# Layer 2 of a four-layer network: turning and weighing move ahead of the projections

## The chip, the cores and the metric

One core of a Trainium2 chip runs the whole program. The metric is device time in microseconds (us) for one execution. A core has five engines that each work through their own instructions in program order and meet only at semaphores: TensorE (PE, matmuls into PSUM), VectorE (DVE), ScalarE (ACT), GpSimd (POOL) and SyncE (SP, which issues transfers).

## The reference

Four layers follow one another, each `x = x + layer(groupnorm(x))`, on 8 images of 32 x 32 tokens with 256 channels. The change is in layer 2, neighbourhood attention with 8 heads of 32 channels and a 7 x 7 window:

```
q, kk, v = split(x @ qkv_w.T + qkv_b)
k_nb, v_nb = the 7 x 7 neighbours of each token (window shifted inside the image)
attn = softmax(einsum('bnijd,bniajcd->bnijac', q * scale, k_nb) + bias)
out = einsum('bnijac,bniajcd->bnijd', attn, v_nb)
out = out @ proj_w.T + proj_b
```

## The kernel before

A tile is 4 x 4 tokens with all 8 heads (128 rows of queries) against the 10 x 10 = 100 keys around it. A step handles 4 tiles, so an image has 16 steps and the layer 128 steps, numbered N over the layer and n within image b. `Tiles` holds the attention pipeline of a step:

- `scores(N)`, TensorE, line 1735: queries against the window of keys, 8 matmuls of 100 columns.
- `add_and_low(N)`, VectorE, line 1773: adds the bias, takes the row extreme; then `exps(N)`, ScalarE, line 1793.
- `invert(N)`, VectorE, line 1779, one step later; then `scale(N)`, GpSimd, line 1800.
- `turn(N)`, TensorE, line 1746, two steps later: transposes the weights into PSUM; `copy_turned(N)`, VectorE, line 1785, copies them to SBUF (PT).
- `weigh(N)`, TensorE, line 1761, three steps later: 32 small matmuls of 16 columns, weights times values, into two PSUM banks that hold half an image.

After 8 weighings ScalarE's `copy_out` (line 2070) moves these banks to `OT`, at n == 10 for the first half and at n == 2 of the next image for the second. The semaphore `o_copied` counts these copies. `weigh` waits for it before the first step of each half (it would overwrite the banks), and `project_out` waits for it before it reads `OT`:

```
if N % (STEPS // 2) == 0 and N > 0:
    pe.wait_ge(self.o_copied, HALVES * (N // (STEPS // 2)))
```

Between the attention work, TensorE does the projections of the next image and the output projection of this one, through a ring of two PSUM banks (`Ring`), one item a step: queries at n = 0, 1 (second half of this image) and 8, 9 (first half of the next), line 1944; the output projection at 3, 4 and 14, 15; values at 4 to 7; keys at 10 to 13 (the last three through helper lines 299 and 307). ScalarE takes the queries out of the ring (`to_blocks`, line 2052, four instructions each) and the values (line 2061), directly behind the exponentials of the same step; VectorE takes the keys (line 2005) and adds the output projection to the residual (line 2012). At n = 0 VectorE measures the next image's group statistics (`moments`, line 384). At the end of step n = 10 and n = 2 ScalarE's order is exponentials, then `copy_out`.

The order of the work on each engine is the order in which these loops are written. Layer 3 uses the same `Tiles`, with its own loop, in which TensorE turns and weighs directly behind the scores and VectorE copies the turned weights before its other work.

Of the kernel before, what the change touches and what calls it, by code (L numbers as in the profile page):

```python
# [11 lines left out]
B, SIDE, C = 8, 32, 256  # L12
# [282 lines left out]
def project(nc, out, w, act, m, n0, n1):  # L295

    tiles = w.shape[1]
    for k in range(tiles):
        i = nc.tensor.matmul(out, w[:, k, m * P:(m + 1) * P], act[:, k, n0:n1], start=(k == 0), stop=(k == tiles - 1))  # L299
    return i  # L300


def project_tokens(nc, out, act, w, t):

    tiles = w.shape[1]
    for k in range(tiles):
        i = nc.tensor.matmul(out, act[:, k, t * P:(t + 1) * P], w[:, k, :], start=(k == 0), stop=(k == tiles - 1))  # L307
    return i
# [122 lines left out]
STEPS = T // TILE ** 2 // STEP  # L431
# [1382 lines left out]
def edge(t):  # L1814
    return 0 if t == 0 else 2 if t == BANDS - 1 else 1
# [26 lines left out]
def layer2(nc, A, x, y, vimg):  # L1842
    with ExitStack() as ctx:
# [16 lines left out]
        w = Tiles(L, keys, SIDE, vimg, 8)  # L1860
# [11 lines left out]
        with nc.Block() as block:  # L1872
            @block.vector
            def _(dve):
                nc.vector.tensor_tensor(bias[:, :, :], bias[:, :, :], window[:, :, :], ALU.add)
                vstep(dve, nc.vector.tensor_scalar(qkv_b[:, 0:HALVES], qkv_b[:, 0:HALVES], HD ** -0.5, None, ALU.mult))
# [8 lines left out]
        with nc.Block() as block:  # L1885
# [41 lines left out]
            @block.tensor  # L1927
            def _(pe):
                def values(b, j):
                    name = ("v", b, j)  # L1930
                    pe.wait_ge(xn_ready, 4 * b + 2 * (j // 2) + 2)
                    ring.may_fill(pe, name)
                    for t in range(2):
                        i = project_tokens(nc, ring.region(name)[:, t * C:(t + 1) * C], xn, wqkv[:, :, 2 * C:3 * C], 2 * j + t)
                    i.then_inc(ring.filled(name), 1)

                def queries(b, half, g):
                    name = ("q", b, half, g)
                    pe.wait_ge(xn_ready, 4 * b + 2 * half + 2)
                    ring.may_fill(pe, name)  # L1940
                    for q in range(4):
                        for k in range(HALVES):
                            band = xn[:, k, (4 * half + q) * P:(4 * half + q + 1) * P]
                            i = nc.tensor.matmul(ring.region(name)[:, q * P:(q + 1) * P], wqkv[:, k, g * P:(g + 1) * P],
                                                 band.rearrange("p (r t c) -> p t r c", r=TILE, c=TILE), start=(k == 0),
                                                 stop=(k == HALVES - 1))
                    i.then_inc(ring.filled(name), 1)

                def unit(name, m, half):
                    pe.wait_ge(xn_ready, 4 * name[1] + 2 * half + 2)  # L1950
                    ring.may_fill(pe, name)
                    project(nc, ring.region(name), wqkv, xn, m, half * BANK, (half + 1) * BANK).then_inc(ring.filled(name), 1)

                def project_out(b, half, m):
                    name = ("out", b, half, m)
                    pe.wait_ge(w.o_copied, 4 * b + 2 * half + 2)
                    ring.may_fill(pe, name)
                    project(nc, ring.region(name), wo, OT, m, half * BANK, (half + 1) * BANK).then_inc(ring.filled(name), 1)

                norm.average(nc, pe, ring, 0)  # L1960
                for j in range(4):
                    values(0, j)
                for g in range(HALVES):
                    queries(0, 0, g)
                for u in range(4):
                    unit(("k", 0, u), HALVES + u % 2, u // 2)
                for N in range(B * STEPS + 3):
                    b, n = N // STEPS, N % STEPS
                    if b < B:
                        if n % 8 == 0:  # L1970
                            for g in range(HALVES):
                                ring.is_taken(pe, ("q", b, n // 8, g))
                        if n == 0:
                            for u in range(4):
                                ring.is_taken(pe, ("k", b, u))
                        w.scores(nc, pe, N)
                        if n < 2:
                            queries(b, 1, n)
                        if n == 1 and b + 1 < B:
                            norm.average(nc, pe, ring, b + 1)  # L1980
                    if n in (3, 4) and 0 < b < B:
                        project_out(b - 1, 1, n - 3)
                    if b + 1 < B:
                        if 4 <= n < 8:
                            values(b + 1, n - 4)
                        if n in (8, 9):
                            queries(b + 1, 0, n - 8)
                        if 10 <= n < 14:
                            unit(("k", b + 1, n - 10), HALVES + (n - 10) % 2, (n - 10) // 2)
                    if n >= 14 and b < B:  # L1990
                        project_out(b, 0, n - 14)
                    if 2 <= N < B * STEPS + 2:
                        w.turn(nc, pe, N - 2)
                    if N >= 3:
                        w.weigh(nc, pe, N - 3)
                for m in range(HALVES):
                    project_out(B - 1, 1, m)

            @block.vector
            def _(dve):  # L2000
                def to_image(b, u):
                    name = ("k", b, u)
                    ring.is_full(dve, name)
                    g, half = u % 2, u // 2
                    nc.vector.tensor_scalar(keys[b % 2][:, g, half * BANK:(half + 1) * BANK], ring.region(name),
                                            qkv_b[:, HALVES + g:HALVES + g + 1], None, ALU.add).then_inc(ring.took(name), 1)

                def residual(b, half, m):
                    name = ("out", b, half, m)
                    ring.is_full(dve, name)  # L2010
                    s = slice(half * BANK, (half + 1) * BANK)
                    nc.vector.scalar_tensor_tensor(norm.x(b)[:, m, s], ring.region(name), proj_b[:, m:m + 1],
                                                   norm.x(b)[:, m, s], ALU.add, ALU.add).then_inc(ring.took(name), 1)

                def table(N, i):
                    _, tr, tc = w.tile(N, i)
                    return bias[:, 3 * edge(tr) + edge(tc), :]

                norm.moments(nc, dve, vstep, 0)
                norm.collect(nc, dve, ring, 0)  # L2020
                for u in range(4):
                    to_image(0, u)
                for N in range(B * STEPS + 2):
                    b, n = N // STEPS, N % STEPS
                    if b < B:
                        w.add_and_low(nc, dve, N, table, 1.0)
                    if 1 <= N < B * STEPS + 1:
                        w.invert(nc, dve, N - 1)
                    if n == 0 and b + 1 < B:
                        norm.moments(nc, dve, vstep, b + 1)  # L2030
                    if n == 1 and b + 1 < B:
                        norm.collect(nc, dve, ring, b + 1)
                    if n in (3, 4) and 0 < b < B:
                        residual(b - 1, 1, n - 3)
                    if 10 <= n < 14 and b + 1 < B:
                        to_image(b + 1, n - 10)
                    if n >= 14 and b < B:
                        residual(b, 0, n - 14)
                    if N >= 2:
                        w.copy_turned(nc, dve, N - 2)  # L2040
                for m in range(HALVES):
                    residual(B - 1, 1, m)

# [785 lines left out]
```

## Time and profile before

| | |
|---|---|
| median of 3 runs | 3466.73 us (3464.69 to 3476.52) |
| profiled execution, its own time | 3469.34 us |
| its span | 3467.5 us |
| mean granted TensorE clock | 0.953 of full speed |
| TensorE matmul busy | 3105.6 us, 90% |
| VectorE busy | 2211.7 us, 64% |
| ScalarE busy | 2058.1 us, 59% |
| GpSimd busy | 1155.1 us, 33% |

The shares are means over four layers with different limits. Layer 2 lies between about 2112 and 2643 us of the span; image 3 in it, for instance, takes the 66 us from 2305 to 2371, with TensorE busy 63.7, ScalarE 40.9, VectorE 33.2 and GpSimd 17.3 us. In rows of time, a row is a start, a length, the engine and line, what is written from what, shapes and a count; what stands in brackets is how long the engine was idle before it and what ended that. A 4-pass matmul of 32-bit numbers counts as two in the trace, so a count there is twice that in the program, but for the transposes. The printed length of a group of matmuls runs a little into the next one; from one start to the next is the safer measure.

### The profile page before, as it was taken

The numbers are of one execution on the slowest core, as the hardware profiler recorded it, in microseconds if no ns is written. First come the engines' busy times: TensorE is split into PE (matmuls) and PEld (weight loads), VectorE is DVE, ScalarE is ACT, GpSimd is POOL, SyncE is SP. The second block draws the span as 40 slices with busy tenths as digits, with TensorE's granted clock in tenths as the row PEclk, the third lists the DMA queues.
The fourth block names the chain that finished last, engine by engine and source line by source line (L and its number), as shares of the span: only waits on it lengthen the run. The fifth ranks groups of instructions, "written<-read, shape, count | busy, mean of one in ns | idle before, by whom it ended". The sixth has DMA issues, their size and how long they took to land. (4 is left out here: it accounts for less than half of the span.)

```text
span 3467.5 us, 94027 instructions
## 1 busy us (share of the span) xinstructions
PE 3105.6 (90%) x38656; PEld 1750.2 (50%) x38656; DVE 2211.7 (64%) x5202; ACT 2058.1 (59%) x4412; POOL 1155.1 (33%) x1446
## 2 busy tenths in 40 slices
PE   6999999999955999999999858999994899999996
PEld 2333333333312556566656526777772566666664
DVE  5878878887733667676777533545543566666765
ACT  2667676767633555545555515656562677777774
POOL 3433434343301222222222202222222455555554
PEclk9999999999976999999999979999997999999998
DMA  6777787777852333323323214445443233333332
GB/s 201 155 173 164 157 184 173 152 174 160 170 130 68 66 86 84 83 72 86 84 71 72 74 57 139 145 143 159 145 133 128 67 93 107 107 113 113 110 95 83
DMA packets 286233, 413.94 MB, mean 119 GB/s; under 512 B 25952, under 2 KB 242800, under 8 KB 264816
## 3 DMA queue, kind: packets, MB, share of 16 engines
q1 hardware_dynamic: 263248, 270.32, 26.0%
q0 software_dynamic: 18432, 134.23, 19.4%
q8 instruction: 308, 5.05, 0.6%
q10 hardware_dynamic: 4128, 3.39, 0.3%
q14 instruction: 117, 0.96, 0.1%
HBM read 219.30 MB, written 53.81 MB: 79 GB/s over the span
## 5 line engine op out<-in xcount | busy, mean ns | idle before, releaser
L732 DVE TENSOR_TENSOR l_probs<-l_psum,l_decay 128x1024 f32<-128x1024 f32 x512 | 598.6, 1219 | 163.5 <-PE l_psum L628 152.8
L780 ACT ACTIVATE l_sizes<-l_probs 128x2048 f32<-128x2048 f32 x256 | 487.6, 1910 | 300.3 <-DVE l_probs L732 293.0
L1793 ACT ACTIVATE l_logits<-l_logits,l_low 128x100 f32<-128x100 f32 x1024 | 374.7, 369 | 238.1 <-DVE l_low L1773 237.1
L1800 POOL TENSOR_TENSOR l_logits<-l_logits,l_inv 128x400 f32<-128x400 f32 x256 | 235.0, 918 | 737.7 <-DVE l_inv L1779 736.8
L628 PE MATMUL l_psum<-l_qk 32*128 32x512 f32 x2048 | 340.6, 646 | 7.9 <-POOL l_qk L866 4.2
L881 POOL DMA_DIRECT2D l_sizes<-l_sizes x128 | 111.5, 871 | 548.1 <-ACT l_sizes L780 536.1
L1632 POOL TENSOR_TENSOR l_E<-l_E,l_causal 128x1024 f32<-128x1024 f32 x64 | 153.3, 2396 | 378.0 <-DVE l_x_act L1365 224.8
L643 PE MATMUL l_psum<-l_probs,l_V 128*32 128x512 f32 x2048 | 270.6, 600 | 1.7 <-DVE l_probs L732 1.6
L299 PE MATMUL l_psum<-l_xT,l_w_up 128*128 128x512 f32 x512 | 232.2, 607 | 12.7 <-DVE l_row_var L1423 8.6
L1735 PE MATMUL l_psum<-l_keys,l_q_blocks 128*64 128x100 f32 x4096 | 230.6, 253 | 3.7 <-issue 2.4
L2726 POOL TENSOR_SCALAR l_soft<-l_dist,l_sharp,l_border 128x100 f32<-128x100 f32 x512 | 229.0, 464 | 0.1
L628 PEld LDWEIGHTS l_psum<-l_qk 32*128 32x128 f32 x2048 | 100.9, 184 | 249.1 <-issue 190.5
L1785 DVE COPY l_PT<-l_psum 100x512 f32<-100x512 f32 x256 | 172.7, 675 | 77.9 <-PE l_psum L1746 76.4
L1761 PE MATMUL l_psum<-l_PT,l_V_windows 100*32 100x16 f32 x16384 | 196.9, 186 | 15.0 <-issue 10.8
L1735 PEld LDWEIGHTS l_psum<-l_keys,l_q_blocks 128*64 128x64 f32 x4096 | 197.5, 136 | 12.6 <-issue 4.8
L1761 PEld LDWEIGHTS l_psum<-l_PT,l_V_windows 100*32 100x32 f32 x16384 | 170.1, 111 | 64.5 <-issue 63.1
L1793 ACT ACTIVATION_READ_ACCUMULATOR l_logits<-l_logits,l_low 128x1 f32 x1024 | 194.4, 190 | 0.0
L1746 PE MATMUL l_psum<-l_ident,l_logits 128*100 128x128 f32 x1024 | 161.6, 281 | 12.0 <-POOL l_logits L1800 11.9
L1773 DVE CUSTOM_DVE_ANT_0 l_logits<-l_psum,l_bias 128x100 f32<-128x100 f32 x512 | 103.3, 258 | 99.5 <-PE l_psum L1735 99.5
L299 PEld LDWEIGHTS l_psum<-l_xT,l_w_up 128*128 128x128 f32 x512 | 97.1, 195 | 125.5 <-issue 121.2
L1500 ACT ACTIVATE l_E<-l_E,l_tok_vals 128x128 f32<-128x128 f32 x512 | 156.5, 396 | 0.9 <-POOL l_E L1632 0.9
L307 PE MATMUL l_psum<-l_w_qkv,l_xn 128*128 128x256 f32 x512 | 130.3, 404 | 18.9 <-DVE l_V L2460 12.8
(246 smaller groups left out, 6072.0 us busy)
## 6 DMA issues: line engine op xcount, KB each, us to landing
l_sizes<-l_sizes POOLq DMA_DIRECT2D x128, 1024.0 KB, 7.5
l_V_windows<-v_image SPq DMA_DIRECT2D x512, 100.0 KB
l_V_windows<-v_padded SPq DMA_DIRECT2D x512, 100.0 KB
l_E<-rows_c SPq DMA_DIRECT2D x64, 512.0 KB, 5.8
l_xT<-y SPq DMA_DIRECT2D x24, 1024.0 KB, 5.3
y<-l_res SPq DMA_DIRECT2D x32, 512.0 KB, 3.7
l_e_everywhere<-rows_e SPq DMA_DIRECT2D x112, 128.0 KB, 5.6
l_xT<-x SPq DMA_DIRECT2D x8, 1024.0 KB, 11.7
```

Of the source, the lines that this page charges most:

```text
L299: i = nc.tensor.matmul(out, w[:, k, m * P:(m + 1) * P], act[:, k, n0:n1], start=(k == 0), stop=(k == tiles - 1))
L628: i = nc.tensor.matmul(out[:, a * BANK:(a + 1) * BANK], qk[r:r + HD, g, 1, J * P:(J + 1) * P], qk[r:r + HD, g, 0, m * BANK:(m + 1) * BANK] ...
L643: i = nc.tensor.matmul(PS[a * HD:(a + 1) * HD, 6 * BANK:7 * BANK], V[:, J, h * HD:(h + 1) * HD], probs[:, N % 2, a, :], start=(J == 0), st ...
L732: nc.vector.tensor_tensor(probs[:, N % 2, 2 * p:2 * p + 2, :], ring.region(name).rearrange("p (a n) -> p a n", a=2), decay[:, h:h + 2, s0: ...
L780: nc.scalar.activation(sizes[:, slot(N), :, :], probs[:, N % 2, :, :], ACT.Abs).then_inc(sized, 1)
L1735: m = nc.tensor.matmul(self.ps[64 * g:64 * g + 64, c0 + i * NKEY:c0 + (i + 1) * NKEY], self.q[:, g, tr * BANDS + tc, :], image[:, r0:r0 + ...
L1746: m = nc.tensor.transpose(self.ps[0:NKEY, c0:c0 + P], self.logits[:, N % 4, i, :], self.ident[:, :])
L1761: m = nc.tensor.matmul(out[:, r0:r0 + TILE, tc * TILE:(tc + 1) * TILE], self.v[0:NKEY, N % self.slots, i, h * HD:(h + 1) * HD], self.pt[0: ...
L1785: nc.vector.tensor_copy(self.pt[0:NKEY, N % 2, :], self.ps[0:NKEY, (2 + N % 2) * BANK:(3 + N % 2) * BANK]).then_inc(self.pt_ready, 1)
L1793: nc.scalar.activation(e, e, ACT.Exp, scale=-1.0, bias=self.low[:, N % 4, i:i + 1], accum_out=self.total[:, N % 4, i:i + 1]).then_inc(self ...
L1800: nc.gpsimd.tensor_tensor(p, p, self.inv[:, N % 4, :].unsqueeze(2).to_broadcast([P, STEP, NKEY]), ALU.mult).then_inc(self.p_ready, 1)
L2726: m = nc.gpsimd.tensor_scalar(soft[:, M % SOFTS, i * NKEY:(i + 1) * NKEY], dist[:, :], sharp[:, b % 2, t:t + 1], border[:, b % 2, t:t + 1] ...
```

## The change

On TensorE, `turn(N - 2)` and `weigh(N - 3)` of a step now stand directly behind `scores(N)`, and the projections of the step last. On VectorE, `copy_turned(N - 2)` stands before the statistics, the keys and the residual of the step.

```diff
                         w.scores(nc, pe, N)
+                    if 2 <= N < B * STEPS + 2:
+                        w.turn(nc, pe, N - 2)
+                    if N >= 3:
+                        w.weigh(nc, pe, N - 3)
+                    if b < B:
                         if n < 2:
                             queries(b, 1, n)
...
                     if n >= 14 and b < B:
                         project_out(b, 0, n - 14)
-                    if 2 <= N < B * STEPS + 2:
-                        w.turn(nc, pe, N - 2)
-                    if N >= 3:
-                        w.weigh(nc, pe, N - 3)
...
                         w.invert(nc, dve, N - 1)
+                    if N >= 2:
+                        w.copy_turned(nc, dve, N - 2)
                     if n == 0 and b + 1 < B:
                         norm.moments(nc, dve, vstep, b + 1)
...
                         residual(b, 0, n - 14)
-                    if N >= 2:
-                        w.copy_turned(nc, dve, N - 2)
```

TensorE before, image 1, steps 8 to 11 (L1735 scores, L1944 queries, L1746 turning, L1761 weighing, L299 keys' projection):

```order
L1735 MATMUL l_psum<-l_keys,l_q_blocks 64x100 x8
L1944 MATMUL l_psum<-l_xn,l_w_qkv 128x128 x8
L1746 MATMUL l_psum<-l_ident,l_logits 100x128 x4
L1761 MATMUL l_psum<-l_PT,l_V_windows 32x4x4 x32
L1735 MATMUL l_psum<-l_keys,l_q_blocks 64x100 x8
L1944 MATMUL l_psum<-l_xn,l_w_qkv 128x128 x8
L1746 MATMUL l_psum<-l_ident,l_logits 100x128 x4
L1761 MATMUL l_psum<-l_PT,l_V_windows 32x4x4 x32
L1735 MATMUL l_psum<-l_keys,l_q_blocks 64x100 x8
L299 MATMUL l_psum<-l_xn,l_w_qkv 128x512 x2
L1746 MATMUL l_psum<-l_ident,l_logits 100x128 x4
L1761 MATMUL l_psum<-l_PT,l_V_windows 32x4x4 x32
```

And TensorE in the same place of the changed kernel:

```order
L1735 MATMUL l_psum<-l_keys,l_q_blocks 64x100 x8
L1746 MATMUL l_psum<-l_ident,l_logits 100x128 x4
L1761 MATMUL l_psum<-l_PT,l_V_windows 32x4x4 x32
L1944 MATMUL l_psum<-l_xn,l_w_qkv 128x128 x8
L1735 MATMUL l_psum<-l_keys,l_q_blocks 64x100 x8
L1746 MATMUL l_psum<-l_ident,l_logits 100x128 x4
L1761 MATMUL l_psum<-l_PT,l_V_windows 32x4x4 x32
L1944 MATMUL l_psum<-l_xn,l_w_qkv 128x128 x8
L1735 MATMUL l_psum<-l_keys,l_q_blocks 64x100 x8
L1746 MATMUL l_psum<-l_ident,l_logits 100x128 x4
L1761 MATMUL l_psum<-l_PT,l_V_windows 32x4x4 x32
L299 MATMUL l_psum<-l_xn,l_w_qkv 128x512 x2
```

In each step the projection has moved from the second place to the last, behind 4 transposes and 32 weighing matmuls.

TensorE before, image 1, from the scores of step 2 to the weighing of step 3 (there L299 is the output projection; step 2 has no projection):

```order
L1735 MATMUL l_psum<-l_keys,l_q_blocks 64x100 x8
L1746 MATMUL l_psum<-l_ident,l_logits 100x128 x4
L1761 MATMUL l_psum<-l_PT,l_V_windows 32x4x4 x32
L1735 MATMUL l_psum<-l_keys,l_q_blocks 64x100 x8
L299 MATMUL l_psum<-l_OT,l_w_proj 128x512 x2
L1746 MATMUL l_psum<-l_ident,l_logits 100x128 x4
L1761 MATMUL l_psum<-l_PT,l_V_windows 32x4x4 x32
```

And TensorE there in the changed kernel:

```order
L1735 MATMUL l_psum<-l_keys,l_q_blocks 64x100 x8
L1746 MATMUL l_psum<-l_ident,l_logits 100x128 x4
L1761 MATMUL l_psum<-l_PT,l_V_windows 32x4x4 x32
L1735 MATMUL l_psum<-l_keys,l_q_blocks 64x100 x8
L1746 MATMUL l_psum<-l_ident,l_logits 100x128 x4
L1761 MATMUL l_psum<-l_PT,l_V_windows 32x4x4 x32
L299 MATMUL l_psum<-l_OT,l_w_proj 128x512 x2
```

Step 2 keeps its order; in step 3 the first instruction that needs `OT`'s copy is now the weighing, where it was the projection.

## Rows read from the trace of the kernel before

**Rows 1.** TensorE's waits in layer 2: who waited for whom, us in total, times, longest.
```profile
PE l_psum L299 <- ACT l_OT L2070: 15.5, 8, 2.2
```

**Rows 2.** TensorE in time, image 1, steps 8 to 11: start us, length us, engine, line.
```profile
2208.41 0.91 PE L1735 MATMUL l_psum<-l_keys,l_q_blocks 128*64 128x100 f32 x16
2209.24 2.05 PE L1944 MATMUL l_psum<-l_xn,l_w_qkv 128*128 128x128 f32 x16
2211.13 0.60 PE L1746 MATMUL l_psum<-l_ident,l_logits 128*100 128x128 f32 x4
...
2212.33 0.91 PE L1735 MATMUL l_psum<-l_keys,l_q_blocks 128*64 128x100 f32 x16
...
2217.09 1.98 PE L299 MATMUL l_psum<-l_xn,l_w_qkv 128*128 128x512 f32 x4
2218.91 0.60 PE L1746 MATMUL l_psum<-l_ident,l_logits 128*100 128x128 f32 x4
2219.44 0.73 PE L1761 MATMUL l_psum<-l_PT,l_V_windows 100*32 100x16 f32 x64
2220.10 0.91 PE L1735 MATMUL l_psum<-l_keys,l_q_blocks 128*64 128x100 f32 x16
```

**Rows 3.** ScalarE in time over the same four steps.
```profile
2209.66 0.38 ACT L1793 ACTIVATE l_logits<-l_logits,l_low 128x100 f32<-128x100 f32 x1 [2.86 <-DVE l_low L1773]
...
2211.33 2.76 ACT L2052 ACTIVATE l_q_blocks<-l_psum,l_qkv_b 32x512 f32<-32x512 f32 x4
...
2215.70 2.76 ACT L2052 ACTIVATE l_q_blocks<-l_psum,l_qkv_b 32x512 f32<-32x512 f32 x4
2218.49 0.38 ACT L1793 ACTIVATE l_logits<-l_logits,l_low 128x100 f32<-128x100 f32 x1
...
2220.23 1.27 ACT L2070 ACTIVATE l_OT<-l_psum,l_qkv_b 128x512 f32<-128x512 f32 x2 [0.17 <-PE l_psum L1761]
```

**Rows 4.** TensorE, then VectorE, in time, image 7, step 15.
```profile
2625.62 0.60 PE L1746 MATMUL l_psum<-l_ident,l_logits 128*100 128x128 f32 x4
...
2625.82 0.75 DVE L2012 SCALAR_TENSOR_TENSOR l_xT<-l_psum,l_proj_b,l_xT 128x512 f32<-128x512 f32 x1 [1.00 <-PE l_psum L299]
```

**Rows 5.** TensorE in time, image 1, from step 0 to step 4.
```profile
2172.03 0.91 PE L1735 MATMUL l_psum<-l_keys,l_q_blocks 128*64 128x100 f32 x16 [0.15 <-issue]
...
2182.28 0.91 PE L1735 MATMUL l_psum<-l_keys,l_q_blocks 128*64 128x100 f32 x16
2185.38 2.98 PE L299 MATMUL l_psum<-l_OT,l_w_proj 128*128 128x512 f32 x4 [2.19 <-ACT l_OT L2070]
...
2189.99 0.91 PE L1735 MATMUL l_psum<-l_keys,l_q_blocks 128*64 128x100 f32 x16
```

**Rows 6.** ScalarE in time, image 1, steps 0 to 3.
```profile
2174.96 2.76 ACT L2052 ACTIVATE l_q_blocks<-l_psum,l_qkv_b 32x512 f32<-32x512 f32 x4
...
2184.06 1.27 ACT L2070 ACTIVATE l_OT<-l_psum,l_qkv_b 128x512 f32<-128x512 f32 x2
```

**Rows 7.** TensorE in time after the same wait in images 2 and 4.
```profile
2252.87 1.98 PE L299 MATMUL l_psum<-l_OT,l_w_proj 128*128 128x512 f32 x4 [1.94 <-ACT l_OT L2070]
...
2384.89 3.78 PE L299 MATMUL l_psum<-l_OT,l_w_proj 128*128 128x512 f32 x4 [2.17 <-ACT l_OT L2070]
```

**Rows 8.** GpSimd, then TensorE, in time, image 0, step 4.
```profile
2124.49 0.85 POOL L1800 TENSOR_TENSOR l_logits<-l_logits,l_inv 128x400 f32<-128x400 f32 x1 [0.87 <-DVE l_inv L1779]
...
2126.15 1.99 PE L307 MATMUL l_psum<-l_w_qkv,l_xn 128*128 128x256 f32 x8 [2.79 <-POOL l_xn L422]
```

**Rows 9.** TensorE in time in layer 3, one step.
```profile
2853.84 0.65 PE L1746 MATMUL l_psum<-l_ident,l_logits 128*100 128x128 f32 x4
2854.42 0.74 PE L1761 MATMUL l_psum<-l_PT,l_V_windows 100*32 100x16 f32 x64
2855.09 1.98 PE L299 MATMUL l_psum<-l_OT,l_w_out 128*128 128x512 f32 x4
2856.91 1.95 PE L2331 MATMUL l_psum<-l_xn,l_w_qkv 128*128 128x128 f32 x16
```

## The prediction

> **What bounds the kernel now.** I read the per-stage windows first, to find where the changed code runs: layer 2 takes about 531 us of the 3467.5 us span (2112 to 2643), and in seven of its eight images TensorE shows some work nearly all the time. So a change of order can win only what TensorE waits for, and can lose where it makes TensorE wait. The list of TensorE's waits over the layer has one entry that matters: the output projection (L299, reading OT) waits eight times, 15.5 us in all, for ScalarE's copy of the weighted values, line 2070 [rows 1]. The rest of the argument comes from the time view.
>
> I count time within an image from the start of the scores of step 0 or of step 8. A step with queries is 0.83 us of scores, 1.89 of queries, 0.53 of turning and 0.67 of weighing, start to start, 3.92 in all; one with a 512-column projection has 1.82 in place of 1.89 and takes 3.85 [rows 2]. TensorE goes from one to the next without a gap. ScalarE has slack in most steps (it waited 2.86 us before the exponentials of step 8), but not in steps 8 to 10 and 0 to 2: there it has two sets of queries to spread into blocks, 2.76 us each, beside its exponentials of about 1.6 us a step and the copy of 1.27 us [rows 3, 6]. Those two stretches decide the case.
>
> **Part 1: the sum of TensorE's own work.** The change adds and removes no instruction. In 110 of the 128 steps (14 in image 0, 15 in each of images 1 to 6, 6 in image 7, counted from the loop) something is projected, and there the neighbours change: before, scores, projection, turning, weighing; after, scores, turning, weighing, projection. Layer 3 already works in the new order, so its rows price it: turning behind scores 0.58, weighing 0.67, projection behind weighing 1.82 [rows 9], against 0.53, 0.66 and 1.82 now [rows 2]. Turning loses 0.05, because its first weight load no longer hides behind a long matmul. Scores now stand behind a long matmul and should win the same; layer 2 has no row for it. I take 0 for the sum. If scores win nothing, it is 110 x 0.05, about +6 us; that is the bound above. The Trainium skill, "TensorE: Matmul & The Clock Gate", section "LDWEIGHTS (loading the stationary operand)", says that a load takes its column count over 1.2 in ns, and its account of a matmul's phases that such a load hides only behind a running matmul; by that a 128-column load behind 16-column weighings costs 107 ns, an estimate of +12 us over 110 steps. Rows 9 show no such surcharge.
>
> **Part 2: steps 8 to 11, where the cost is new.** Queries are usable 0.20 us after the next instruction group starts (the same delay shows at a residual, 2625.62 to 2625.82 [rows 4]). Before, the first queries land at 0.83 + 1.89 + 0.20 = 2.92 us, exactly when ScalarE, whose exponentials began at 1.25, turns to them [rows 2, 3]. After, they land behind turning and weighing: 0.83 + 0.57 + 0.67 + 1.89 + 0.20 = 4.16. ScalarE takes its work in program order, so it idles 1.24 us with the exponentials of step 9 queued behind. Then: blocks 4.16 to 6.92; exponentials of step 9 to 8.53; blocks (the second queries land at 3.92 + 4.16 = 8.08) to 11.29; exponentials of step 10, 1.57, to 12.9; copy 1.27, to 14.17. TensorE needs that copy for the first weighing of the second half of the image, since it overwrites what the copy reads. That weighing stands in step 11, whose scores start at 11.69 [rows 2]. Before, it comes at 11.69 + 0.84 + 1.82 + 0.53 = 14.88 and the copy is over at 11.82 + 1.27 = 13.09: 1.8 us to spare, nothing waits. After, it comes at 11.69 + 0.84 + 0.57 = 13.10 and the copy is done at 14.17, seen 0.05 later: a new wait of about 1.15 us. (In the old order the copy itself waited for the last weighing of step 10 [rows 3]; that one comes earlier now, but ScalarE is not free to use it.) It happens in images 0 to 6: **+8.0 us**. ScalarE has its slack back by step 12.
>
> **Part 3: steps 0 to 3.** The same delay of 1.24 us enters at the first queries (ScalarE starts them at 2.93 now, and would at 4.16), and nothing up to the copy absorbs it: ScalarE runs without a break from there to 13.30 [rows 6]. VectorE's scores of step 1 are held by the group statistics of step 0, but those end near 5.5, before ScalarE's 6.9. Before: the copy ends at 13.30, the projection of step 3 starts at 13.35 after a wait of 2.2, and at full clock 1.82 + 0.53 + 0.67 follow, so step 4 could start at 16.37 [rows 5]. After: scores and turning of step 3 are over at 10.25 + 0.83 + 0.57 = 11.65; now the weighing waits for the copy, until 14.59, 2.9 us; 0.67 and 1.82 follow, so step 4 starts at 17.08. Turning moved ahead of the wait gives 0.53 back, the delay takes 1.24: 0.71 net, in images 1 to 7: **+5.0 us**.
>
> **Part 4: the ends.** In image 0, step 4, values wait for the normalised input until 2126.15, and turning and weighing stand behind them [rows 8]. After, turning starts when GpSimd's scaling is over (2125.34, plus 0.05), weighing ends at 2126.63, and values follow: 2126.63 against 2126.15 + 1.20, **-0.7 us**. At the layer's end the last residual, 0.75 us [rows 4], stands right before the last reciprocal, which the last turning needs: up to **+0.7 us**. VectorE's copy of the turned weights moves ahead of its projection work; TensorE waits for it nowhere now, so that gives 0. The projection work behind it reads 1.2 us later and ends at about 4.85 in its step, when the next scores are ready (4.80): covered to 0.05 us. The value stores and the window loads on SyncE are tied to values copied a step earlier and to weighings that come earlier: 0.
>
> **Part 5: the clock.** After the wait in image 1 the four projection matmuls take 2.98 us, and step 4 starts 4.61 us after them where 3.02 would do: 1.6 lost at the lower of the clock's two levels, 1.2 instead of 2.4 GHz. In image 4 they take 3.78; in image 2, after 1.94 of wait, 1.98, full clock [rows 5, 7]. By the same subtraction five of the seven images lose, 9.0 us in all by my reading of the time view. With 2.9 us of wait I expect it in nearly all seven: 7 x 1.8 = 12.6, at most +3.6, and I take **+2 us**.
>
> **Sum:** 8.0 + 5.0 - 0.7 + 0.7 + 0 + 2 = **+15 us**. The profiled execution took 3469.3 us beside a median of 3466.7; so 3484 on its scale, and 3482 as a median.
>
> **Rivals.**
> Dearer order (0.13): the clock also falls after the seven new waits of 1.15 us (7 x 1.6 = +11), or the scores win nothing and weight loads show (+6). For it: waits of about 2.2 us do it. Against: they are twice as long, and rows 9 are clean. Time 3488 to 3498.
> Clock given back (0.14): the waits move to other places, and the 9.0 us lost to the clock now are not lost again. 13 - 9 = +4: 3471, no change to be seen. For it: image 2 waited 1.94 without loss. Against: the waits get longer.
> ScalarE absorbs the delay (0.07), the one that ends faster: if the 1.24 us did not reach the copy, turning ahead of the wait gives 7 x 0.53, the wait of step 3 shrinks to 1.7 and the clock stays up (9.0), and step 11 doesn't wait: -13, so 3454. Step 3 changes sign where less than 0.53 us of delay reaches the copy. Only slack on ScalarE could do that, and in steps 0 to 2 the trace shows none.
> No effect (0.05): TensorE's total counts alone; 3467.
>
> **The numbers.** Forecast 0.61. The measurement tells a change from none at about 0.3%, 10.4 us, that is 3477. The forecast's own range is 3474 to 3488, since the sum without the clock is +13 and small terms can miss: about nine tenths of it is slower. Slower 0.61 x 0.9 + 0.13, about 0.68; same 0.06 + 0.14 + 0.05, about 0.25; faster 0.07. The range of 3464 to 3496 leaves out the faster rival and the top of the dearer one.
>
> **What would show it.** TensorE's waits: a new entry, weighing (L1761) waiting for OT's copy, fourteen times, 7 x 1.15 and 7 x 2.9, some 28 us; no projection waiting for OT except at the layer's end. ScalarE: about 1.2 us of waiting for queries (L1944) ahead of the first block copy of each pair. VectorE: reads of keys and residuals start 0.2 us after the next scores. I am wrong if the weighing of step 11 doesn't wait, if step 4 doesn't start near 17, or if a step of plain projection takes other than 3.85 us.

## The result

The changed kernel is slower: 3492.1 us as the median of 5 runs (3486.6 to 3499.7), beside 3473.3 us for the kernel before in 5 runs (3464.7 to 3476.6). The ratio is 1.0064, with a 95% interval of 1.0037 to 1.0091, so about +22 us (+13 to +32); the two medians are 18.9 us apart. That is beyond the 0.3% bound, on the side that was forecast, inside the range of 3464 to 3496, and more than the +15 of the sum: 3492.1 lies above the forecast's own 3474 to 3488 and within the 3488 to 3498 of the dearer-order rival.

The profile after, its span, TensorE's share and the row of the weighing:

```profile
span 3484.8 us, 94027 instructions
...
PE 3107.6 (89%) x38656; PEld 1737.2 (50%) x38656; DVE 2207.2 (63%) x5202; ACT 2053.2 (59%) x4412; POOL 1154.6 (33%) x1446
...
L1761 PE MATMUL l_psum<-l_PT,l_V_windows 100*32 100x16 f32 x16384 | 196.4, 186 | 38.4 <-ACT l_OT L2071 23.7
```

Over the whole program TensorE is as busy as before (3107.6 against 3105.6 us) and there are as many instructions; within layer 2 alone it is busier, 510.6 us after 497.0 (in a second pair of traces 509.5 after 494.4). New in the weighing's row is 23.7 us of idle time that ScalarE's copy to OT (now line 2071) ended.

Single runs of one kernel differ by some 0.3%, and layer 2 begins anywhere between 2098.9 and 2122.7 us in the traces below, so from here on I compare the length of layer 2 alone: from the first scores to the start of the last residual. Before it is 526.6 us (2112.23 to 2638.82), after 547.6 us (2106.10 to 2653.72): +21.0 us, and layers 0 and 1 together and layer 3 differ by 6 us the one way and 2 the other. So layer 2 alone accounts for the effect.

TensorE's waits there, as in [rows 1]:

```profile
PE l_psum L1761 <- ACT l_OT L2071: 23.7, 14, 2.8
...
PE l_psum L1746 <- POOL l_logits L1800: 3.3, 3, 2.0
PE l_psum L299 <- ACT l_OT L2071: 1.4, 1, 1.4
```

Fourteen waits of the weighing have taken the place of seven of the eight of the output projection; the eighth, at the layer's end, stays. TensorE over image 1, steps 8 to 11, then two steps further on one whole step with a keys' projection (compare [rows 2]):

```profile
2206.25 0.91 PE L1735 MATMUL l_psum<-l_keys,l_q_blocks 128*64 128x100 f32 x16
...
2210.44 0.91 PE L1735 MATMUL l_psum<-l_keys,l_q_blocks 128*64 128x100 f32 x16
...
2214.69 0.91 PE L1735 MATMUL l_psum<-l_keys,l_q_blocks 128*64 128x100 f32 x16
...
2218.68 0.91 PE L1735 MATMUL l_psum<-l_keys,l_q_blocks 128*64 128x100 f32 x16
2219.52 0.64 PE L1746 MATMUL l_psum<-l_ident,l_logits 128*100 128x128 f32 x4
2220.68 0.73 PE L1761 MATMUL l_psum<-l_PT,l_V_windows 100*32 100x16 f32 x64 [0.52 <-ACT l_OT L2071]
...
2227.40 0.91 PE L1735 MATMUL l_psum<-l_keys,l_q_blocks 128*64 128x100 f32 x16
2228.24 0.64 PE L1746 MATMUL l_psum<-l_ident,l_logits 128*100 128x128 f32 x4
2228.81 0.73 PE L1761 MATMUL l_psum<-l_PT,l_V_windows 100*32 100x16 f32 x64
2229.48 1.98 PE L299 MATMUL l_psum<-l_xn,l_w_qkv 128*128 128x512 f32 x4
2231.39 0.91 PE L1735 MATMUL l_psum<-l_keys,l_q_blocks 128*64 128x100 f32 x16
```

ScalarE over the same steps (compare [rows 3]; the bracket is the new wait for the queries):

```profile
2210.55 2.75 ACT L2053 ACTIVATE l_q_blocks<-l_psum,l_qkv_b 32x512 f32<-32x512 f32 x4 [1.48 <-PE l_psum L1944]
...
2214.91 2.76 ACT L2053 ACTIVATE l_q_blocks<-l_psum,l_qkv_b 32x512 f32<-32x512 f32 x4
...
2219.27 1.27 ACT L2071 ACTIVATE l_OT<-l_psum,l_qkv_b 128x512 f32<-128x512 f32 x2
```

The copy ends at 2219.27 + 1.27 = 2220.54, 14.29 us after the scores of step 8, where 14.17 was forecast. But the wait of step 11 is 0.52 and not 1.15 us, because TensorE is late itself: its step 11 starts 12.43 us after step 8, not 11.69. The last five rows show the cause of 0.14 us in each step (the other 0.3 us here are two longer weighings in steps 8 and 9, such as single steps of both kernels have). From scores to scores it takes 3.99 us, not 3.85: scores 0.84, turning 0.57, weighing 0.67 and the projection **1.91**, where it took 1.82.

TensorE in steps 0 to 4 of image 1 (compare [rows 5]), then ScalarE's first query copy and its copy to OT (compare [rows 6]):

```profile
2170.49 0.91 PE L1735 MATMUL l_psum<-l_keys,l_q_blocks 128*64 128x100 f32 x16
...
2180.81 0.91 PE L1735 MATMUL l_psum<-l_keys,l_q_blocks 128*64 128x100 f32 x16
...
2185.12 0.73 PE L1761 MATMUL l_psum<-l_PT,l_V_windows 100*32 100x16 f32 x64 [2.83 <-ACT l_OT L2071]
...
2187.69 0.91 PE L1735 MATMUL l_psum<-l_keys,l_q_blocks 128*64 128x100 f32 x16
```

```profile
2174.66 2.76 ACT L2053 ACTIVATE l_q_blocks<-l_psum,l_qkv_b 32x512 f32<-32x512 f32 x4 [1.35 <-PE l_psum L1944]
...
2183.71 1.27 ACT L2071 ACTIVATE l_OT<-l_psum,l_qkv_b 128x512 f32<-128x512 f32 x2
```

The weighing of step 3 waits 2.83 us (2.9 forecast) and step 4 starts 17.20 us after step 0 (17.08 forecast).

### The profile page after: what moved, and what is told of

The parts are those of the page before. It is cut to its first block and busy times, and to the rows that moved or that the text cites. A ratio compares the mean times of both kernels' runs of the same rounds, so it can differ in the third digit from the quotient of the medians.

```text
span 3484.8 us, 94027 instructions
## 1 busy us (share of the span) xinstructions
PE 3107.6 (89%) x38656; PEld 1737.2 (50%) x38656; DVE 2207.2 (63%) x5202; ACT 2053.2 (59%) x4412; POOL 1154.6 (33%) x1446
## 5 line engine op out<-in xcount | busy, mean ns | idle before, releaser
L299 PE MATMUL l_psum<-l_xT,l_w_up 128*128 128x512 f32 x512 | 231.6, 606 | 13.1 <-DVE l_row_var L1423 8.8
L1735 PE MATMUL l_psum<-l_keys,l_q_blocks 128*64 128x100 f32 x4096 | 230.9, 254 | 0.9 <-DVE l_keys L2006 0.9
L1761 PE MATMUL l_psum<-l_PT,l_V_windows 100*32 100x16 f32 x16384 | 196.4, 186 | 38.4 <-ACT l_OT L2071 23.7
L1735 PEld LDWEIGHTS l_psum<-l_keys,l_q_blocks 128*64 128x64 f32 x4096 | 198.0, 137 | 58.9 <-issue 51.7
L1761 PEld LDWEIGHTS l_psum<-l_PT,l_V_windows 100*32 100x32 f32 x16384 | 170.5, 111 | 88.0 <-issue 66.2
L1746 PE MATMUL l_psum<-l_ident,l_logits 128*100 128x128 f32 x1024 | 166.1, 285 | 14.2 <-POOL l_logits L1800 14.2
L299 PEld LDWEIGHTS l_psum<-l_xT,l_w_up 128*128 128x128 f32 x512 | 96.9, 194 | 125.9 <-issue 121.7
L652 PE MATMUL l_psum<-l_sizes,l_ones 128*32 128x512 f32 x1024 | 138.0, 611 | 9.5 <-DMA l_sizes<-l_sizes 9.5
## 6 DMA issues: line engine op xcount, KB each, us to landing
l_e_everywhere<-rows_e SPq DMA_DIRECT2D x112, 128.0 KB, 5.6
```

Of the source, the lines that this page charges most:

```text
L1735: m = nc.tensor.matmul(self.ps[64 * g:64 * g + 64, c0 + i * NKEY:c0 + (i + 1) * NKEY], self.q[:, g, tr * BANDS + tc, :], image[:, r0:r0 + ...
L1746: m = nc.tensor.transpose(self.ps[0:NKEY, c0:c0 + P], self.logits[:, N % 4, i, :], self.ident[:, :])
L1761: m = nc.tensor.matmul(out[:, r0:r0 + TILE, tc * TILE:(tc + 1) * TILE], self.v[0:NKEY, N % self.slots, i, h * HD:(h + 1) * HD], self.pt[0: ...
```

## The experiments

Layer 2 in the trace of each kernel, in the order in which they are told:

| kernel | layer 2, us | ratio to the kernel before |
|---|---|---|
| before, first and second trace | 526.6, 522.3 | |
| changed, first and second trace | 547.6, 547.4 | 1.0064 [1.0037, 1.0091] |
| e3: queries early | 550.3 | 1.0065 [1.0038, 1.0093] |
| e4: turning last | 563.9 | 1.0095 [1.0063, 1.0128] |
| e5: wide first load | 565.2 | one run, no interval |
| e1: VectorE's half alone | 540.4 | 1.0060 [1.0039, 1.0081] |
| e9: the same, not at n = 0 | 519.2 | 1.0004 [0.9982, 1.0026] |
| e2: TensorE's half alone | 554.4 | 1.0076 [1.0053, 1.0099] |
| e8: queries early, their copy late | 533.2 | 1.0040 [1.0020, 1.0060] |
| e7: changed, copy to OT first | 529.5 | 1.0035 [1.0019, 1.0050] |
| e6: before, copy to OT first | 512.4 | 0.9960 [0.9947, 0.9974] |

**The two kernels again.**

> The kernel before, once more, to see how much the length of layer 2 (from the first scores to the start of the last residual, 526.6 us in the first trace) differs from one execution to the next. Both theories expect 524 to 530: the granted clock after the seven waits for OT's copy is the only thing that should differ.

> The changed kernel once more. Layer 2 took 547.6 us in the first trace; 544 to 551 expected, again with steps of 3.99 us and with fourteen waits of the weighing for OT's copy.

Layer 2 took 522.3 and 547.4 us, so the difference is 21 to 25 us, and a single length is good to some 5 us. What differs most between the two traces of before is the granted clock behind the wait for OT's copy. In the first trace it fell to the lower of its two levels in five of the seven images (1, 3, 4, 5 and 6), in the second in one (3); image 1 did not lose there, after nearly the same wait of 2.17 us:

```profile
2183.53 1.99 PE L299 MATMUL l_psum<-l_OT,l_w_proj 128*128 128x512 f32 x4 [2.17 <-ACT l_OT L2070]
```

Compare the 2.98 us of this row's twin in [rows 5]. In the changed kernel it fell behind the wait in four of the seven images in the first trace (2, 3, 5, 6) and in five in the second (2, 3, 4, 6, 7).

**e3: only the queries early.**

```diff
                         w.scores(nc, pe, N)
+                        if n < 2:
+                            queries(b, 1, n)
+                        if n in (8, 9) and b + 1 < B:
+                            queries(b + 1, 0, n - 8)
                     if 2 <= N < B * STEPS + 2:
                         w.turn(nc, pe, N - 2)
```

The same calls are taken out behind the weighing.

> The changed kernel, with the queries alone (n = 0, 1, 8, 9) put back directly behind the scores; all other projections stay last. Theory ScalarE: the queries land at 2.9 us again, so the seven waits of step 11 go (4.4 us), and the waits of step 3 shrink from 2.8 to about 1.7 us (8 us). Theory weight load: the 30 query steps go back from 4.06 to 3.92 (4 us), the other 80 keep 3.99. With both at work layer 2 takes about 531 us; with the second alone 543; with the first alone 535.

```profile
PE l_psum L1761 <- ACT l_OT L2071: 20.2, 7, 3.4
```

The waits of step 11 are gone (7 are left of 14), and query steps are back at 3.92 us: both theories have their piece. But layer 2 is 550.3 us, not 531, and the wait of step 3 has grown to 3.4 us instead of shrinking. So something else makes step 3 late here. It took e1 to see what: VectorE's copy, moved ahead, waits for turning in step 0, and the scores of step 1 are read late.

**e4: turning last in the step.**

```diff
                         w.scores(nc, pe, N)
-                    if 2 <= N < B * STEPS + 2:
-                        w.turn(nc, pe, N - 2)
                     if N >= 3:
                         w.weigh(nc, pe, N - 3)
...
                     if n >= 14 and b < B:
                         project_out(b, 0, n - 14)
+                    if 2 <= N < B * STEPS + 2:
+                        w.turn(nc, pe, N - 2)
```

> The changed kernel, with turning put last in the step: scores, weighing, projection, turning. Theory weight load: a projection followed by scores costs 0.09 us more than one followed by turning, since the 64-column weights of the scores are not loaded behind it as the 100-column ones of turning are; so steps are 3.86 us again although the projection still stands behind the weighing, 15 us less; the waits for OT's copy stay, about 1.2 us in step 11 and 2.9 in step 3: layer 2 about 540 us. Rival, that it is the projection behind the weighing that costs (its first load has only 16-column matmuls to hide behind): steps stay at 3.99, layer 2 about 552.

One step of it on TensorE:

```profile
2214.27 0.91 PE L1735 MATMUL l_psum<-l_keys,l_q_blocks 128*64 128x100 f32 x16
2215.13 0.74 PE L1761 MATMUL l_psum<-l_PT,l_V_windows 100*32 100x16 f32 x64
2215.79 1.99 PE L307 MATMUL l_psum<-l_w_qkv,l_xn 128*128 128x256 f32 x8
2217.62 0.60 PE L1746 MATMUL l_psum<-l_ident,l_logits 128*100 128x128 f32 x4
2218.16 0.91 PE L1735 MATMUL l_psum<-l_keys,l_q_blocks 128*64 128x100 f32 x16
```

The step is 3.89 us from scores to scores (2214.27 to 2218.16), with 1.83 for the values' projection that stands behind the weighing, and 3.87 is the sum for a keys' step. So the projection's place behind the weighing costs nothing; what costs is that scores follow it. For that question the run is clean. The total of 563.9 is far over the 540 expected: the waits for OT's copy grew to 33.4 us and the granted clock fell behind the wait of step 3 in all seven images. The reason is that of e3, which e1 shows below: VectorE's copy stands first and turning now comes last in the step, so the scores of step 1 in image 1, begun at 2188.35, are read only at 2192.19. I had not put that into the expectation.

**e5: a full-width load at the head of the scores.** In each step of layer 2 the first score matmul takes 128 columns of weights, its tile's 64 and the next tile's; the next matmul overwrites the upper half of the output.

```diff
+                wide = self.side == SIDE and i == g == 0
-                m = nc.tensor.matmul(self.ps[64 * g:64 * g + 64, c0 + i * NKEY:c0 + (i + 1) * NKEY],
-                                     self.q[:, g, tr * BANDS + tc, :], image[:, r0:r0 + KEYS, k0:k0 + KEYS],
+                m = nc.tensor.matmul(self.ps[0:P, c0 + i * NKEY:c0 + (i + 1) * NKEY] if wide else
+                                     self.ps[64 * g:64 * g + 64, c0 + i * NKEY:c0 + (i + 1) * NKEY],
+                                     self.q[:, g, tr * BANDS + tc:tr * BANDS + tc + 2, :].rearrange("p t q -> p (t q)") if wide
+                                     else self.q[:, g, tr * BANDS + tc, :], image[:, r0:r0 + KEYS, k0:k0 + KEYS],
```

> The changed kernel, but in layer 2 the first score matmul of each step takes 128 columns of weights (its tile and the next) instead of 64; the second matmul overwrites the half that isn't wanted. Theory weight load, in the form that a load is only pulled ahead where it has the width of the one in use: a projection followed by scores goes from 1.91 back to about 1.82 us, the scores themselves may grow by up to 0.06: layer 2 538 to 545 us. Rival: the cost has another cause (the change of the PSUM bank or of the operand): 1.91 stays, layer 2 547 to 552.

The load of that first matmul, then TensorE from a projection to turning:

```profile
2233.40 0.19 PEld L1736 LDWEIGHTS l_psum<-l_keys,l_q_blocks 128*128 128x128 f32 x1 [0.24 <-issue]
...
2232.01 1.98 PE L299 MATMUL l_psum<-l_xn,l_w_qkv 128*128 128x512 f32 x4
2233.83 1.19 PE L1736 MATMUL l_psum<-l_keys,l_q_blocks 128*128 128x100 f32 x16
2234.95 0.64 PE L1749 MATMUL l_psum<-l_ident,l_logits 128*100 128x128 f32 x4
```

The load (2233.40) starts 0.43 us ahead of its matmul (2233.83), as the load of turning does before. The projection is back at 1.82. Without this edit, in the changed kernel:

```profile
2230.44 0.19 PEld L299 LDWEIGHTS l_psum<-l_xn,l_w_qkv 128*128 128x128 f32 x1 [0.24 <-issue]
2231.39 0.28 PEld L1735 LDWEIGHTS l_psum<-l_keys,l_q_blocks 128*64 128x64 f32 x6 [0.76 <-issue]
```

the 64-column load starts only with its matmul, 2231.39, after 0.76 us in which nothing was loaded; the median over the layer is the same, for scores behind a projection of keys or output. And in the kernel before, the load of turning behind the same projection, whose matmul starts at 2230.47:

```profile
2230.04 0.13 PEld L1746 LDWEIGHTS l_psum<-l_ident,l_logits 128*100 128x100 f32 x1 [0.24 <-issue]
```

So the difference of 0.09 us is one hidden weight load. Weights of the projection and of turning go to all 128 output partitions or to 100 of them, those of the scores to 64; a load behind a projection was pulled ahead for turning (before) and for the widened scores (e5) and not for the scores of 64. That the width decides is the plainest reading, since e5 keeps the bank and the operand and changes only how many output columns the load takes; no run varies the width further. As a repair it is worthless: the scores with the wide first matmul are 1.12 us long in place of 0.84 (2233.83 to 2234.95), 0.28 us more where I had allowed 0.06, and layer 2 takes 565.2 us in this one run.

**e1: VectorE's half alone.**

```diff
                         w.invert(nc, dve, N - 1)
+                    if N >= 2:
+                        w.copy_turned(nc, dve, N - 2)
                     if n == 0 and b + 1 < B:
                         norm.moments(nc, dve, vstep, b + 1)
```

> The kernel before, with VectorE's half of the change alone: the copy of the turned weights ahead of statistics, keys and residual. My theory: TensorE waits for that copy nowhere, so nothing changes, layer 2 524 to 530 us. Rival: the copy stands ahead of the keys and the residual, so with turning late in the step it waits for turning, and these come later; if something hangs on them, layer 2 gets longer by up to 0.1 us in each of 60 steps.

My theory was wrong: 540.4 us, and 1.0060. VectorE in step 0 of image 1 (scores at 2177.35 are those of step 1):

```profile
2176.79 0.69 DVE L1785 COPY l_PT<-l_psum 100x512 f32<-100x512 f32 x1 [1.51 <-PE l_psum L1746]
2177.40 2.46 DVE L384 BATCH_NORM_STATS2 l_gn_stats<-l_xT 128x6 f32<-128x512 f32 x4
...
2180.53 0.26 DVE L1773 CUSTOM_DVE_ANT_0 l_logits<-l_psum,l_bias 128x100 f32<-128x100 f32 x1
```

```profile
PE l_psum L299 <- ACT l_OT L2070: 19.4, 8, 3.2
```

The copy waits for turning, which in the old TensorE order stands last, and the group statistics (2.46 us) stand behind it. So the scores of step 1 are read at 2180.53, 3.18 us after they were begun. Before it was 1.53 us, and that was just when ScalarE became free [rows 6]. The output projection of step 3 then waits up to 3.2 us. The rival had the right direction but not the place.

**e9: the same, but not at n = 0** (diff against the kernel before).

```diff
                         w.invert(nc, dve, N - 1)
+                    if N >= 2 and n not in (0,):
+                        w.copy_turned(nc, dve, N - 2)
...
-                    if N >= 2:
+                    if N >= 2 and n in (0,):
                         w.copy_turned(nc, dve, N - 2)
```

> The kernel before with VectorE's half of the change in all steps but n = 0. If all the loss of VectorE's half alone (layer 2 540.4 against 526.6 and 522.3 us) comes from the statistics of step 0 that wait behind the copy, this takes 522 to 528 us. Rival, that the copy ahead of keys and residual costs something in other steps too: 530 to 540.

519.2 us and a ratio of 1.0004: the loss of e1 came from step 0. Ahead of the keys and the residual the copy costs nothing that can be seen here.

**e2: TensorE's half alone.**

> TensorE's half of the change alone; VectorE copies the turned weights last as before. VectorE reads keys and residuals about 4.2 us after the step's scores start, so its copy ends near 5.6, and the weighing of the next step stands at 5.4: my theory expects a new wait of about 0.25 us in each step with keys or output projection, 50 to 60 of them, so layer 2 about 560 us. Rival: the copy is in time anyway, and the two halves of the change are independent: 547 us as with both.

(VectorE's two moved lines are put back where they were.)

```profile
PE l_psum L1761 <- ACT l_OT L2071: 21.8, 14, 2.6
...
PE l_psum L1761 <- DVE l_PT L1785: 3.1, 7, 1.0
```

554.4 us, 7 more than with both halves. The seven waits of the second row are six of 0.3 to 0.4 us in step 1, behind the statistics of step 0, and one of 1.0 at the layer's end. The wait that I expected in the steps behind keys or a residual is there too, but it is only 0.10 us, too short for that list. Image 4, step 12, turning and weighing, then VectorE's copy between them:

```profile
2380.18 0.64 PE L1746 MATMUL l_psum<-l_ident,l_logits 128*100 128x128 f32 x4
2380.85 0.90 PE L1761 MATMUL l_psum<-l_PT,l_V_windows 100*32 100x16 f32 x64
...
2380.12 0.68 DVE L1785 COPY l_PT<-l_psum 100x512 f32<-100x512 f32 x1
```

The copy ends at 2380.80 and the weighing starts at 2380.85, 0.67 us after turning; with both halves it is 0.57. The longer distance stands in 40 steps (n = 12 to 15 and 0 nearly throughout, a few at 4), 4.0 us; with six times 0.36 and the 1.0 that is the 7 us. So the mechanism was right and its size, 0.25 us, was not; the rival, that the halves are independent, is refuted.

**e8: e3 with VectorE's old order in the query steps.** VectorE's part of the edit, against e3:

```diff
-                    if N >= 2:
+                    if N >= 2 and n not in (0, 1, 8, 9):
                         w.copy_turned(nc, dve, N - 2)
...
                     if n >= 14 and b < B:
                         residual(b, 0, n - 14)
+                    if N >= 2 and n in (0, 1, 8, 9):
+                        w.copy_turned(nc, dve, N - 2)
```

> The changed kernel, with query steps (n = 0, 1, 8, 9) wholly in the order of before, on TensorE and on VectorE: in these steps VectorE copies the turned weights last again. The earlier run with TensorE's half of this alone took 550.3 us; theory: there the copy stood ahead of the statistics of step 0 and waited for turning, so the scores of step 1 were read 1.9 us late. Then this one has no wait in step 11, a wait of at most 1.8 us in step 3, steps of 3.99 us in the 80 others (+11 us): layer 2 524 to 534 us. Rival, that queries early don't help since ScalarE isn't the cause: 545 to 551.

```profile
PE l_psum L1761 <- ACT l_OT L2073: 11.2, 7, 1.7
```

533.2 us, and no wait of step 3 above 1.7 where 1.8 was the most expected: as expected. This is the changed kernel without the delay of the queries. It is 14 us shorter than the changed one and 9 longer than the mean of before (524.4). What remains is about what the 80 steps of 3.99 us cost, 11 us.

**e7 and e6: the copy to OT ahead of the exponentials at n = 2**, in the changed kernel (e7) and in the kernel before (e6).

```diff
                     b, n = N // STEPS, N % STEPS
+                    if n == 2 and b > 0:
+                        copy_out(2 * b - 1)
                     w.exps(nc, act, N)
```

> The changed kernel with the copy to OT ahead of the exponentials at n = 2. If ScalarE's queue sets the wait of the weighing in step 3, the copy ends near 13.0 us after step 0 started and not near 14.5, so seven waits fall from 2.8 to about 1.3 us: 10 us less, and fewer drops of the clock behind them; layer 2 530 to 537 us, and the steps keep 3.99 and the waits of step 11 their 0.6 us. Against the same move in the kernel before (layer 2 512.4) it stays about 20 us longer: 15 for the steps, 4 for step 11. Rival, that the weighing waits for something else: 545 to 550.

> The kernel before, with one move on ScalarE: at n = 2 the copy to OT stands ahead of the step's exponentials. If ScalarE's queue is what the output projection of step 3 waits for, the copy starts when the last weighing is over (about 10.4 us after step 0 started) and ends near 11.7, so the wait falls from 2.2 to about 0.6 us, 7 times: -11 us, and the clock doesn't fall behind it, up to 9 more: layer 2 507 to 517 us. Rival: the exponentials of step 2 are then late and hold the turning of step 4: the wait only moves, layer 2 524 to 528.

In e7 the same fourteen waits fell from 23.7 to 12.8 us, the longest from 2.8 to 1.4:

```profile
PE l_psum L1761 <- ACT l_OT L2071: 12.8, 14, 1.4
```

and layer 2 from 547.5 to 529.5 us; the granted clock fell behind none of the seven waits of step 3, where it had fallen behind four and five. In e6 ScalarE's second query copy, its copy to OT and the projection of step 3 in image 1, and the waits of the layer:

```profile
2178.51 2.75 ACT L2052 ACTIVATE l_q_blocks<-l_psum,l_qkv_b 32x512 f32<-32x512 f32 x4
...
2181.75 1.26 ACT L2070 ACTIVATE l_OT<-l_psum,l_qkv_b 128x512 f32<-128x512 f32 x2
...
2183.07 1.98 PE L299 MATMUL l_psum<-l_OT,l_w_proj 128*128 128x512 f32 x4 [0.88 <-ACT l_OT L2070]
```

```profile
PE l_psum L299 <- ACT l_OT L2070: 6.0, 8, 1.4
```

The copy starts 0.5 us after the query copy ends. The eight waits are 6.0 us where they were 15.5, none of the seven projections of step 3 runs at the lower clock, and layer 2 takes 512.4 us. The kernel takes 3452.3 us (median of 6) beside 3467.2 (13 runs), ratio 0.9960 with an interval of 0.9947 to 0.9974. It beats both kernels. e7 against e6 leaves 17 us for what TensorE's order costs beside the wait of step 3, where 20 were expected; since in e6 the clock also fell in step 4 of image 0 (9.12 us for 6.72) and in e7 it did not, 19 to 20 us is the better figure.

## Why the prediction was right, and where it was not

**Part 1, the sum of TensorE's own work: the term that was mis-sized.** I took 0, with +6 above. It measured +0.14 us a step: turning +0.04 as read from layer 3, the projection +0.09 (1.91 for 1.82), and no gain on the scores (0.84 stays), where I had expected them to win back what turning lost. Over 110 steps that is +15 us, beyond my bound (14 us with step 15, whose weighing took 0.82 us before and 0.67 after, so that this step stayed at 4.0 in images 0 to 6; why it was longer before is not shown). A step of plain projection of 3.99 us for 3.85 is one of the three signs by which the prediction was to be called wrong; the other two, the wait of step 11 and step 4 near 17, came as forecast. The rows of e4 and e5 show why: behind a projection the load of turning is hidden and that of the scores is not, so what turning loses nobody wins. The changed order has one hidden load less in every step. My row for the projection (2855.09 to 2856.91 [rows 9]) had another full-width matmul behind it, while in the changed layer the scores stand there. I had priced a group by what stands ahead of it and had not asked what stands behind it. The rule of the Trainium skill weighed there ("TensorE: Matmul & The Clock Gate", section "LDWEIGHTS (loading the stationary operand)") was applied to the projection behind the weighing; the estimate of +12 us from it comes close to the measured 15, but from another place: e4 shows 1.82 to 1.83 in that position, no surcharge.

**Part 2, steps 8 to 11: right in mechanism, too large in size.** The wait is where it was put, the copy ends within 0.12 us of the forecast, and e3 and e8 remove it. It is 0.5 to 0.7 us, not 1.15, so 4.5 us in all for 8.0 (23.7 less seven of 2.6 to 2.8). TensorE's own longer steps, which part 1 had put at nothing, hide the rest.

**Part 3, steps 0 to 3: right.** 2.6 to 2.8 us of wait for 2.9; step 4 at 17.20 for 17.08, so 0.83 us more an image than the 16.37 of an undisturbed one before, 5.8 us for 5.0. e8 shows that the delay of the queries is its cause, and e6 and e7 that ScalarE's queue is. The statement (in part 4) that VectorE's copy, moved ahead, "gives 0" held only together with TensorE's half, where it saves 7 us (e2); by itself it costs 14 to 18 us (e1).

**Part 4, the ends: nearly.** The last output projection starts 11.98 us after the scores of step 15, before 10.47 (in the second traces 11.95 and 10.57): +1.4 to +1.5 where +0.7 was the most. The last residual follows at 17.13 and before at 15.86, but at 17.11 and 17.05 in the second pair: there the clock was low for longer in the kernel before, and from that projection to the residual it took 6.48 us, beside 5.15 to 5.39 in the other three traces. In image 0 turning does wait for GpSimd's scaling, 2.04 us, and where the clock stayed up step 4 takes 5.97 us (second trace of the changed kernel) for 6.72 (first trace of before): the -0.7 as forecast. In each of the other two traces the clock fell there, and it took 8.67 and 9.21.

**Part 5, the clock: open in size.** In the kernel before, the waits of step 3 (1.6 to 2.2 us in the first trace, 1.2 to 2.3 in the second) were followed by the lower clock in five of seven images and in one; in the changed kernel the waits of 2.6 to 2.8 us were in four and in five, not in nearly all seven as expected. Steps 0 to 3 of images 1 to 7 took 2.9 us more in the first pair of traces (125.8 for 122.9) and 12.9 more in the second (128.0 for 115.2), where 5.8 would do without the clock. So the clock was worth about -3 us in one pair and +7 in the other. Their mean is the +2 that was taken, but two pairs 10 us apart cannot confirm it.

Put together at full clock: of the 89 steps outside steps 0 to 3 of images 1 to 7 all but seven steps 15 at 0.14, 11.5 us; step 11, 4.5; steps 0 to 3, 5.8; the end, 1.4; image 0, -0.7; together some 22 us. With the clock as it fell (-3 in images 1 to 7 and +2.7 in image 0 in the first pair; +7, -2.5 and, at the layer's end, -1.3 in the second) that gives 22 and 26, against 21.0 and 25.2 in the traces. The prediction's +15 is some 7 short of this, and that it came so near is in part luck, since misses partly cancelled: TensorE's own work 11.5 too low where it shows, steps 0 to 3 and the end 1.5 too low, step 11 3.5 too high (linked to the first, since longer steps eat waits), and 2 for the clock, which this sum leaves out.

**The rivals.** "Dearer order" was true in its second half (weight loads show), not in its first (no lower clock behind the short waits). Its time, 3488 to 3498, holds the measured one. "ScalarE absorbs the delay" is refuted by the copy's end at 14.29 us for 14.17 and by e8; "clock given back" and "no effect" by the measured slowdown.

## What to carry to other kernels

When instructions change places on TensorE, price each neighbourhood anew, the pair behind as well as the pair ahead: here the same four groups in another order cost 0.14 us more a step, since one weight load lost its cover, and the steps with a projection made most of the loss. When one engine's work moves later within a step, follow it into the engine that takes it up, and look for the stretch in which that engine has no slack: 1.2 us of delay there came out whole. And before an order is rewritten, look at the releaser of the largest wait: moving that one copy ahead of four exponentials gave 0.4% where reordering TensorE lost 0.6%.

## What the runs showed of the hardware

- A weight load for 64 output columns was not started while a 128-wide projection ran (load and matmul both at 2231.39, loader idle 0.76 us); one for 128 (e5) and one for 100 (turning) was, 0.43 us ahead. One matmul with 128 columns of weights ahead of seven with 64 made the scores 0.28 us longer (e5), more than the hidden load gave back (0.09).
- The same wait of 2.17 to 2.19 us was followed by projections at the lower clock (2.98 us) in one execution and at the full clock (1.99 us) in another.
- Two halves of a change, 6 and 7.6 thousandths slower each by itself, cost 6.4 thousandths together: they are not additive. With VectorE's half alone its copy waits 1.51 us for turning, and the statistics behind it come late (e1); with TensorE's half alone the weighing waits for the copy (e2).
